# Shorter lags and another order of phases in the second attention's software pipeline

## The chip, the cores and the metric

The kernel runs on one core of one Trainium2 chip. The core has five engines with one instruction queue each: TensorE (PE in the profile; its weight loads are PEld), VectorE (DVE), ScalarE (ACT), GpSimd (POOL) and SyncE (SP, which here only issues DMAs). Each queue is worked off in its own order, and the queues wait for each other on semaphores. The metric is the device time of one launch in microseconds (us).

## The reference, cut to what matters

The program is one transformer chain on x of 32 sequences x 64 tokens x 256 features: a gated expert FFN, a hyperbolic attention, a typed expert FFN, a second attention with a router behind it, and a mixture-of-experts FFN. The change is in the second attention and its router:

```
x = x + _attn(x, ln1_w, ln1_b, conv_w, attn_w, proj_w, n_head)      # 16 heads of 16, RoPE, causal softmax
# inside _moe, what runs in the same stage of the kernel:
h = _layernorm(x, ln_w, ln_b)
logits = h @ router_w
expert_idx = jnp.argmax(logits, axis=-1)
```

## The kernel before, in words

`attention` is called twice, with the tag `hyp` (hyperbolic) and with the tag `rope` (the second attention; `hyper` is False). Its second half treats 16 blocks of 128 tokens (two sequences each) as items of a software pipeline. An item i goes through some 25 phases on five engines. The table `lag` says in which step of the pipeline: a phase of lag L treats item i in step i + L. The table `order` says in which order an engine issues its phases within a step. `run` issues steps 0 to `first` - 1 one by one, then a loop of two steps a turn up to step 15, then the remaining steps to 15 + the largest lag. With the largest lag 9 there are 25 steps, of which the loop holds 12 to 15. Most buffers are double, by the parity of the item.

The phases of the second attention, by engine, with the line that does the work:

- PE: `turn` (transposes of k, L1147, and q, L1153), `score` (q times k, L1169), `p_turn` (transposes of the probabilities, L1177), `mix` (probabilities times v, L1188), `y_turn` (L1200), `out` (output projection and residual, L1209 and L1211), `h_turn` (transposes of the normalised rows, L1227), `route` (router logits, L1239).
- ACT: copies out of PSUM, `q_blk` (L1251), `p_take` (L1284), `y_take` (L1289), `x2` (the sum x, L1295), `h_take` (L1309); `prob` (exponential, L1279); `rstd` (1/sqrt of the variance, two instructions, L1301 and L1303).
- DVE: `k_blk` (k spread into blocks by head, L1332), `clamp` (scale and causal mask, L1343), `top` (row maximum, L1354), `y` (division by the sum, L1360 and L1368), `stats` and `aggr` (mean and variance, L1380 and L1388), `keep` (logits to SBUF, L1393). Behind the last item `router.choose` (from L704 on) picks the experts.
- POOL: `shift` (minus the maximum, L1417), `total` (L1428), `norm` (L1432), `weigh` (L1438), `lift` (L1444). The last four make an item's rows for the expert stage.
- SP: loads `bring` (q and k, L1111), `fetch` (v, L1105), `bring_sum` (residual, L1116), `bring_x` (L1121) and `store` (rows to DRAM, L1127).

What the steps of the argument wait for: `h_turn(i)` waits for `lift(i)` and shares a PSUM bank with q's transposes; `total(i)` waits for `rstd(i)`, which waits for `aggr(i)`; `x2(i)` waits for `out(i)`; `q_blk(i)` waits for q's transposes of i; `score(i)` for `q_blk(i)`, `k_blk(i)` and `clamp(i-1)`; `out(i)` also for `bring_sum(i)`; `fetch(i)` for `mix(i-2)`, since it overwrites its buffer; and `p_turn(i)` for `prob(i)`. In the loop `score`'s waits stand on the last matmul of `route` (`score_ready`). The expert stage begins behind a barrier of all engines.

Of the kernel before, what the change touches and what calls it, by code (L numbers as in the profile page):

```python
# [17 lines left out]
KC = D // P  # L18
# [7 lines left out]
NP = N // P  # L26
# [687 lines left out]
def attention(nc, m, tag, hyper, srcT, resT, w, router=None, stored=None):  # L714
# [14 lines left out]
    with ExitStack() as s:  # L729
# [295 lines left out]
        if hyper:  # L1025
            lag = dict(turn=0, q_blk=0, k_blk=0, score=0, clamp=1, root_sq=1, root_ln=2, root=2, root_add=2, dist_ln=2,
                       dist=3, mask=3, top=3, shift=3, prob=4, p_turn=4, p_take=4, mix=5, y=5, y_turn=5, y_take=6,
                       out=6, add=6, stretch=0, fetch=3)
            order = dict(tensor="mix out turn p_turn y_turn score",
                         scalar="y_take dist root_ln prob root q_blk root_sq p_take dist_ln",  # L1030
                         vector="stretch clamp y add k_blk top", gpsimd="mask root_add shift", sync="fetch")
        else:
            lag = dict(bring=0, turn=1, q_blk=1, k_blk=1, score=1, clamp=2, top=2, shift=2, prob=2, p_turn=3, p_take=3,
                       mix=3, y=3, y_turn=4, y_take=4, out=4, fetch=2, bring_sum=3, bring_x=5, x2=4, stats=5, aggr=5, rstd=5,
                       total=5, norm=5, weigh=5, lift=5, h_turn=8, h_take=8, route=9, keep=9, store=7)
            order = dict(tensor="h_turn y_turn p_turn turn out mix route score",
                         scalar="y_take h_take p_take rstd q_blk x2 prob",
                         vector="stats clamp top aggr k_blk y keep", gpsimd="shift total norm weigh lift",
                         sync="bring fetch bring_sum bring_x store")
        last = max(lag.values())  # L1040
        sem = StageSemaphores(nc, tag)
# [14 lines left out]
        with ExitStack() as s2:  # L1056
# [42 lines left out]
            with nc.Block() as block:  # L1099
# [34 lines left out]
                def _(pe):  # L1134
                    def turn(i, q, nth):


                        if hyper:
                            pe.wait_ge(stretched, i + 1)
                        else:  # L1140
                            pe.wait_ge(brought[q], 16 * (nth + 1))
                        chunk = lambda n: x[:, q, n * P:(n + 1) * P]
                        wait(pe, k_blocked, i)
                        if not hyper:
                            wait(pe, kept, i + lag["turn"] - lag["route"])
                        for c in range(KC):
                            ins = pe.transpose(kT_ps[:, c * P:(c + 1) * P], chunk(KC + c), m.ident)  # L1147
                        ins.then_inc(k_turned, 1)
                        wait(pe, q_taken, i)
                        if not hyper:  # L1150
                            wait(pe, h_taken, i + lag["turn"] - lag["h_turn"] + 1)
                        for c in range(KC):
                            ins = pe.transpose(qT_ps[:, c * P:(c + 1) * P], chunk(c), m.ident)  # L1153
                        ins.then_inc(turned, 1)
# [26 lines left out]
                    def mix(i, q, nth):  # L1181

                        pe.wait_ge(p_taken, i + 1)
                        pe.wait_ge(v_fetched[q], 16 * (nth + 1))
                        wait(pe, y_scaled, i)
                        for hp in range(HP):
                            for j in range(2):
                                ins = pe.matmul(y_ps[j * T:(j + 1) * T, hp * 2 * VW:(hp + 1) * 2 * VW],  # L1188
                                                pT[:, q, hp, j * T:(j + 1) * T],
                                                v_now[:, q, j, hp].rearrange("p h v -> p (h v)"), start=True, stop=True)  # L1190
                        ins.then_inc(mixed, 1)
# [28 lines left out]
                    def h_turn(i, q, nth):  # L1220

                        pe.wait_ge(lifted, i + 1)
                        wait(pe, h_taken, i)
                        behind = i + lag["h_turn"] - lag["turn"]
                        wait(pe, q_taken, behind if not isinstance(i, int) else min(behind, NP))
                        for c in range(KC):
                            ins = pe.transpose(hT_ps[:, c * P:(c + 1) * P], router.rows[:, q, c * P:(c + 1) * P], m.ident)  # L1227
                        ins.then_inc(h_turned, 1)

                    def route(i, q, nth):  # L1230

                        pe.wait_ge(h_taken, i + 1)
                        wait(pe, kept, i)
                        behind = i + lag["route"] - lag["turn"] + 1
                        wait(pe, k_blocked, behind if not isinstance(i, int) else min(behind, NP))
                        for c in range(KC):
                            if not isinstance(i, int) and c == KC - 1:
                                score_ready(i + lag["route"] - lag["score"])
                            ins = pe.matmul(lg_ps, router.hT[:, q, c], router.wr[:, c], start=(c == 0), stop=(c == KC - 1))  # L1239
                        ins.then_inc(routed, 1)  # L1240

# [1200 lines left out]
```

## Time and profile before

| | us |
|---|---|
| median of 3 runs (2227.89 to 2228.91) | 2228.83 |
| the profiled execution's own time | 2227.89 |
| its span | 2226.1 |
| PE busy in the span | 2035.3 (91%) |
| DVE, ACT, POOL busy | 1106.0, 935.9, 720.6 |
| second attention's pipeline, first transposes to the last logits' copy | 1875.7 to 1987.4 |

The span is cut by stage: the pipeline of the second attention takes some 112 us of it, 5%. Busy shares of the whole program say little of it; its own stretch has to be read. Starts in the rows are us from the span's start.

### The profile page before, as it was taken

How to read it: one execution, taken by the hardware profiler on the slowest of the kernel's cores; microseconds unless marked ns; L12 is line 12 of the kernel's file. 1: busy time of each engine (PE TensorE's matmuls, PEld its weight loads, DVE VectorE, ACT ScalarE, POOL GpSimd, SP SyncE). 2: the span in 40 equal slices, each digit the busy share in tenths (PEclk: the TensorE clock that was granted, in tenths of full speed). 3: DMA queues.
4: the chain of work that ended last, by engine and by line, in shares of the span. 5: the costliest groups of instructions: out<-in, count | busy, mean ns of one | idle time of the engine just before them, and what ended most of it. 6: DMA issues, size and time to landing. Idle time of an engine off the chain costs nothing. (4 is left out here: it accounts for less than half of the span.)

```text
span 2226.1 us, 32462 instructions
## 1 busy us (share of the span) xinstructions
PE 2035.3 (91%) x11700; PEld 1717.9 (77%) x11700; DVE 1106.0 (50%) x1946; ACT 935.9 (42%) x1916; POOL 720.6 (32%) x777
## 2 busy tenths in 40 slices
PE   7999999999999999999998767799899765968998
PEld 6888888888888888888887545678699734858998
DVE  3334433443343344344344787333377574856775
ACT  4242323324233232323323599322255354645664
POOL 3030200203021020302200198202178314868884
PEclk9999999999999999999999798999999877978999
DMA  4010010101001010110000200320056303446661
GB/s 162 1 57 1 1 57 0 57 0 51 6 0 57 0 57 0 39 43 0 1 1 19 67 31 37 117 76 10 0 182 208 103 16 109 172 165 214 211 216 55
DMA packets 97922, 144.50 MB, mean 65 GB/s; under 512 B 15567, under 2 KB 72817, under 8 KB 97841
## 3 DMA queue, kind: packets, MB, share of 16 engines
q1 hardware_dynamic: 90784, 127.42, 17.7%
q0 software_dynamic: 4928, 12.86, 1.6%
q10 hardware_dynamic: 2128, 3.15, 0.4%
q8 instruction: 50, 0.82, 0.1%
q14 instruction: 32, 0.25, 0.0%
HBM read 109.32 MB, written 12.06 MB: 55 GB/s over the span
## 5 line engine op out<-in xcount | busy, mean ns | idle before, releaser
L584 DVE TENSOR_TENSOR cond_h<-cond_silu,ps 128x512 f32<-128x512 f32 x288 | 198.1, 688 | 696.5 <-ACT cond_silu L495 693.1
L495 ACT ACTIVATE cond_silu<-ps 128x512 f32<-128x512 f32 x288 | 172.3, 598 | 771.7 <-PE ps L414 771.7
L414 PE MATMUL ps<-a_x_hi,cond_w_hi 128*128 128x512 f32 x1152 | 449.3, 390 | 2.0 <-DVE a_x_lo L262 2.0
L414 PE MATMUL ps<-a_x_lo,cond_w_hi 128*128 128x512 f32 x1152 | 448.9, 390 | 0.0
L414 PE MATMUL ps<-a_x_hi,cond_w_lo 128*128 128x512 f32 x1152 | 448.7, 390 | 0.0
L383 POOL TENSOR_TENSOR cond_w_lo<-cond_stage_up,cond_w_hi 128x256 fp32r<-128x256 f32 x144 | 108.6, 772 | 832.3 <-ACT cond_w_hi L476 832.3
L414 PEld LDWEIGHTS ps<-a_x_hi,cond_w_hi 128*128 128x128 f32 x1152 | 216.7, 188 | 47.3 <-DVE a_x_lo L262 2.4
L414 PEld LDWEIGHTS ps<-a_x_hi,cond_w_lo 128*128 128x128 f32 x1152 | 216.6, 188 | 45.2
L414 PEld LDWEIGHTS ps<-a_x_lo,cond_w_hi 128*128 128x128 f32 x1152 | 216.7, 188 | 44.9
L430 PE MATMUL ps<-cond_h_hi,cond_d_hi 128*128 128x512 f32 x576 | 224.5, 390 | 3.4 <-DVE cond_h_lo L552 3.4
L430 PE MATMUL ps<-cond_h_hi,cond_d_lo 128*128 128x512 f32 x576 | 224.1, 389 | 0.0
L430 PE MATMUL ps<-cond_h_lo,cond_d_hi 128*128 128x512 f32 x576 | 224.1, 389 | 0.0
L552 DVE TENSOR_TENSOR cond_h_lo<-cond_h,cond_h_hi 128x512 fp32r<-128x512 f32 x288 | 199.7, 694 | 0.1
L489 ACT ACTIVATE cond_h_hi<-cond_h 128x512 fp32r<-128x512 f32 x288 | 179.6, 624 | 0.3 <-DVE cond_h L584 0.3
L430 PEld LDWEIGHTS ps<-cond_h_hi,cond_d_hi 128*128 128x128 f32 x576 | 108.1, 188 | 27.4 <-issue 2.4
L430 PEld LDWEIGHTS ps<-cond_h_hi,cond_d_lo 128*128 128x128 f32 x576 | 108.1, 188 | 22.6
L430 PEld LDWEIGHTS ps<-cond_h_lo,cond_d_hi 128*128 128x128 f32 x576 | 108.1, 188 | 22.3
L2024 POOL TENSOR_TENSOR moe_w_lo<-moe_stage_up,moe_w_hi 128x512 fp32r<-128x512 f32 x88 | 113.0, 1302 | 29.2 <-ACT moe_w_hi L2130 28.8
L555 DVE SCALAR_TENSOR_TENSOR dense_h_lo<-ps,dense_h_hi 128x512 fp32r<-128x512 f32 x64 | 44.2, 692 | 123.0 <-ACT dense_h_hi L501 123.0
L2077 PE MATMUL ps<-moe_x_hi,moe_w_hi 128*128 128x256 f32 x352 | 100.9, 287 | 1.4 <-DVE moe_x_lo L2185 1.4
L2077 PE MATMUL ps<-moe_x_lo,moe_w_hi 128*128 128x256 f32 x352 | 100.6, 286 | 0.0
L2077 PE MATMUL ps<-moe_x_hi,moe_w_lo 128*128 128x256 f32 x352 | 100.6, 286 | 0.0
(369 smaller groups left out, 4105.4 us busy)
## 6 DMA issues: line engine op xcount, KB each, us to landing
moe_stage_up<-in_L_ffn_expert_wv SPq DMA_DIRECT2D x22, 1024.0 KB, 8.2
typed_stage_up<-in_L_cond_wi SPq DMA_DIRECT2D x11, 1024.0 KB, 4.9
typed_stage_dn<-in_L_cond_wo SPq DMA_DIRECT2D x11, 1024.0 KB, 5.9
moe_stage_dn<-in_L_ffn_expert_proj SPq DMA_DIRECT2D x11, 1024.0 KB, 6.8
cond_stage_up<-in_L_cond_Wg SPq DMA_DIRECT2D x7, 1024.0 KB, 4.8
cond_stage_up<-in_L_cond_Wu SPq DMA_DIRECT2D x7, 1024.0 KB, 6.8
cond_stage_dn<-in_L_cond_Wd SPq DMA_DIRECT2D x7, 1024.0 KB, 5.4
hyp_v_now<-hyp_v_blk SPq DMA_DIRECT2D x16, 272.0 KB, 2.3
```

Of the source, the lines that this page charges most:

```text
L383: ins = pool.tensor_tensor(w_lo[:, j, :, c], stage_up[:, j, :, c], w_hi[:, j, :, c], ALU.subtract)
L414: ins = pe.matmul(up_ps[st % 2][j], w[:, j, k, fs], x[:, k, tok], start=(i == 0), stop=(i == 3 * KC - 1))
L430: ins = pe.matmul(y_ps[tt % 2][c], w[:, f, cs], x[:, st % HB], start=(f == 0 and i == 0), stop=(f == FC - 1 and i == 2))
L489: act.activation(h_hi[:, st % HB], h[:, st % 2], ACT.Copy).then_inc(h_rounded, 1)
L495: act.activation(silu[:, st % 2], up_ps[st % 2][0], ACT.Silu).then_inc(act_done, 1)
L552: dve.tensor_tensor(h_lo[:, st % HB], h[:, st % 2], h_hi[:, st % HB], ALU.subtract).then_inc(h_ready, 1)
L555: dve.scalar_tensor_tensor(h_lo[:, st % HB], up_ps[st % 2][0], 0.0, h_hi[:, st % HB], ALU.max, ALU.subtract).then_inc(h_ready, 1)
L584: dve.tensor_tensor(h[:, st % 2], silu[:, st % 2], up_ps[st % 2][1], ALU.mult).then_inc(up_free, 1)
L2024: pool.tensor_tensor(w_lo[:, :, :, fs(f)], stage_up[:, q, :, :, fs(f)], w_hi[:, :, :, fs(f)], ALU.subtract).then_inc(up_ready, 1)
L2077: ins = pe.matmul(up_ps[f % UB][j], w[:, j, k, fs(f)], x[:, q, k], start=(i == 0), stop=(i == 3 * KC - 1))
```

## The change

For the second attention alone, `lag` and `order` are other numbers and words. The lags of the router's phases fall (`h_turn` and `h_take` 8 to 6, `route` and `keep` 9 to 6, `store` 7 to 6), those of `fetch` 2 to 1 and `bring_x` 5 to 4. The largest lag is then 6: 22 steps, of which the loop holds 8 to 15. On PE `out` comes before `turn`, `h_turn` behind `p_turn`, `score` before `route`. On ACT `x2` and `q_blk` come before `rstd`. On DVE `clamp` comes before `stats`. In the loop `score`'s waits stand on the last matmul of `mix`. The waits that guard shared PSUM banks are written with the numbers that the new lags ask for.

```diff
-            lag = dict(bring=0, ..., fetch=2, bring_sum=3, bring_x=5, x2=4, stats=5, aggr=5, rstd=5,
-                       total=5, norm=5, weigh=5, lift=5, h_turn=8, h_take=8, route=9, keep=9, store=7)
-            order = dict(tensor="h_turn y_turn p_turn turn out mix route score",
-                         scalar="y_take h_take p_take rstd q_blk x2 prob",
-                         vector="stats clamp top aggr k_blk y keep", gpsimd="shift total norm weigh lift",
+            lag = dict(bring=0, ..., fetch=1, bring_sum=3, bring_x=4, x2=4, stats=5, aggr=5, rstd=5,
+                       total=5, norm=5, weigh=5, lift=5, h_turn=6, h_take=6, route=6, keep=6, store=6)
+            order = dict(tensor="y_turn p_turn h_turn out turn mix score route",
+                         scalar="y_take p_take h_take x2 q_blk rstd prob",
+                         vector="clamp stats top aggr k_blk y keep", gpsimd="shift total norm weigh lift",
...
-                            wait(pe, kept, i + lag["turn"] - lag["route"])
+                            wait(pe, kept, i - 5)
...
-                            wait(pe, h_taken, i + lag["turn"] - lag["h_turn"] + 1)
+                            wait(pe, h_taken, i - 4)
...
+                                if not hyper and not isinstance(i, int) and (hp, j) == (HP - 1, 1):
+                                    score_ready(i + lag["mix"] - lag["score"])
                                 ins = pe.matmul(y_ps[j * T:(j + 1) * T, hp * 2 * VW:(hp + 1) * 2 * VW],
...
-                        wait(pe, q_taken, behind if not isinstance(i, int) else min(behind, NP))
+                        wait(pe, q_taken, i + 5 if not isinstance(i, int) else min(i + 5, NP))
...
-                        wait(pe, k_blocked, behind if not isinstance(i, int) else min(behind, NP))
+                        wait(pe, k_blocked, i + 6 if not isinstance(i, int) else min(i + 6, NP))
                         for c in range(KC):
-                            if not isinstance(i, int) and c == KC - 1:
-                                score_ready(i + lag["route"] - lag["score"])
                             ins = pe.matmul(lg_ps, router.hT[:, q, c], router.wr[:, c], start=(c == 0), stop=(c == KC - 1))
```

ACT's queue in one full step, written out ahead of the loop. Before (`router_x2` is written by `x2`, `rope_qT` by `q_blk`, `router_rstd` by `rstd`):

```order
L1289 ACTIVATE rope_yT<-ps 128x256
L1309 ACTIVATE router_hT<-ps 128x256
L1284 ACTIVATE rope_pT<-ps 128x1024
L1301 ACTIVATE router_rstd<-router_mean,router_eps 128x1
L1303 ACTIVATE router_rstd<-router_rstd 128x1
L1251 ACTIVATE rope_qT<-ps 128x256
L1295 ACTIVATE router_x2<-ps 128x256
L1279 ACTIVATE rope_prob<-rope_u 128x1024
```

and now:

```order
L1287 ACTIVATE rope_yT<-ps 128x256
L1282 ACTIVATE rope_pT<-ps 128x1024
L1307 ACTIVATE router_hT<-ps 128x256
L1293 ACTIVATE router_x2<-ps 128x256
L1249 ACTIVATE rope_qT<-ps 128x256
L1299 ACTIVATE router_rstd<-router_mean,router_eps 128x1
L1301 ACTIVATE router_rstd<-router_rstd 128x1
L1277 ACTIVATE rope_prob<-rope_u 128x1024
```

The two instructions of `rstd` moved from ahead of `q_blk` and `x2` to behind both, and `router_hT` from ahead of `rope_pT` to behind it.

PE's queue in one full step. Before (`router_rows` is read by `h_turn`, `rope_x` by `turn`, `router_hT` by `route`):

```order
L1227 MATMUL ps<-const,router_rows 128x128 x2
L1200 MATMUL ps<-const,rope_y 128x128 x2
L1177 MATMUL ps<-const,rope_prob 128x128 x8
L1147 MATMUL ps<-const,rope_x 128x128 x2
L1153 MATMUL ps<-const,rope_x 128x128 x2
L1209 MATMUL ps<-rope_wo,rope_yT 128x256 x2
L1211 MATMUL ps<-const,router_res 128x128 x2
L1188 MATMUL ps<-rope_v_now,rope_pT 64x34 x16
L1239 MATMUL ps<-router_wr,router_hT 128x4 x2
L1169 MATMUL ps<-rope_k_blk,rope_qT 64x256 x8
```

and now:

```order
L1202 MATMUL ps<-const,rope_y 128x128 x2
L1177 MATMUL ps<-const,rope_prob 128x128 x8
L1228 MATMUL ps<-const,router_rows 128x128 x2
L1211 MATMUL ps<-rope_wo,rope_yT 128x256 x2
L1213 MATMUL ps<-const,router_res 128x128 x2
L1147 MATMUL ps<-const,rope_x 128x128 x2
L1153 MATMUL ps<-const,rope_x 128x128 x2
L1190 MATMUL ps<-rope_v_now,rope_pT 64x34 x16
L1169 MATMUL ps<-rope_k_blk,rope_qT 64x256 x8
L1237 MATMUL ps<-router_wr,router_hT 128x4 x2
```

`h_turn` moved from the front of the step to just ahead of `out`, and the item that it transposes is that of six steps ago, not of eight. `turn` stands behind `out`.

SP's queue at the pipeline's start, now:

```order
L1111 DMA rope_x<-rope_qk 128x512
L1105 DMA rope_v_now<-rope_v_blk 128x544
L1116 DMA router_res<-sum 128x2x128
L1111 DMA rope_x<-rope_qk 128x512
L1105 DMA rope_v_now<-rope_v_blk 128x544
L1116 DMA router_res<-sum 128x2x128
L1121 DMA router_x<-typed_table 128x256
```

The kinds of rows stand in the same order as before; what moved is the item of `rope_v_now` in a step (one later than before), and with it the `mix` that the row waits for, and all rows behind it.

## Rows read from the trace of the kernel before

**Rows 1.** Windows: steady part and drain; busy us (instructions), granted clock, DMA share.

```profile
core 0: us, PE busy (x) PEld busy (x) DVE busy (x) ACT busy (x) POOL busy (x), PEclk, DMA share, GB/s
1900.00:1965.40 65.40, 64.36 (x852) 54.14 (x848) 53.23 (x88) 42.25 (x88) 59.52 (x58) 1.00 0.49 171
1965.40:1987.40 22.00, 17.19 (x160) 14.87 (x156) 6.56 (x21) 9.12 (x24) 17.41 (x20) 0.86 0.34 116
```

**Rows 2.** Timeline, PE, one step in the loop: start, us, line, xcount, [idle before].

```profile
1941.95 0.44 PE L1227 MATMUL ps<-const,router_rows 128*128 128x128 f32 x2
1942.23 0.38 PE L1200 MATMUL ps<-const,rope_y 128*128 128x128 f32 x2
1942.44 1.04 PE L1177 MATMUL ps<-const,rope_prob 128*128 128x128 f32 x8
1943.32 0.38 PE L1147 MATMUL ps<-const,rope_x 128*128 128x128 f32 x2
...
1943.76 1.03 PE L1209 MATMUL ps<-rope_wo,rope_yT 128*128 128x256 f32 x4
...
1945.16 1.13 PE L1188 MATMUL ps<-rope_v_now,rope_pT 128*64 128x34 f32 x32
1946.21 0.61 PE L1239 MATMUL ps<-router_wr,router_hT 128*128 128x4 f32 x4
1946.75 1.09 PE L1169 MATMUL ps<-rope_k_blk,rope_qT 64*64 64x256 f32 x16
1947.78 0.44 PE L1227 MATMUL ps<-const,router_rows 128*128 128x128 f32 x2
```

**Rows 3.** Timeline, ACT, same step, one copy behind another.

```profile
1945.32 0.38 ACT L1251 ACTIVATE rope_qT<-ps 128x256 f32<-128x256 f32 x1
1945.60 0.38 ACT L1295 ACTIVATE router_x<-ps 128x256 f32<-128x256 f32 x1
```

**Rows 4.** Timeline, DVE and POOL, next step.

```profile
1948.00 1.23 DVE L1343 SCALAR_TENSOR_TENSOR rope_u<-ps,const 128x1024 f32<-128x1024 f32 x1 [0.17 <-PE ps L1169]
...
1949.42 1.22 DVE L1354 TENSOR_REDUCE rope_mx<-rope_u 128x16 f32<-128x1024 f32 x1 [0.19 <-DVE rope_u L1343]
...
1950.72 1.90 POOL L1417 TENSOR_TENSOR rope_u<-rope_u,rope_mx 128x1024 f32<-128x1024 f32 x1 [0.50 <-DVE rope_mx L1354]
...
1952.58 0.73 POOL L1428 TENSOR_TENSOR router_rows<-router_x 128x256 f32<-128x256 f32 x1
...
1955.40 0.73 POOL L1444 TENSOR_TENSOR router_rows<-router_xn,router_b 128x256 f32<-128x256 f32 x1
```

**Rows 5.** Timeline: hops from engine to engine, first in step 4, then in the drain.

```profile
1890.80 0.44 PE L1200 MATMUL ps<-const,rope_y 128*128 128x128 f32 x2
...
1891.27 0.38 ACT L1289 ACTIVATE rope_yT<-ps 128x256 f32<-128x256 f32 x1 [0.17 <-PE ps L1200]
...
1973.21 0.28 ACT L1301 ACTIVATE router_rstd<-router_mean,router_eps 128x1 f32<-128x1 f32 x1
...
1973.98 0.72 POOL L1428 TENSOR_TENSOR router_rows<-router_x 128x256 f32<-128x256 f32 x1 [0.46 <-ACT router_rstd L1303]
```

**Rows 6.** Timeline: k's blocks on DVE and the scores that wait for them.

```profile
1882.20 1.21 DVE L1332 TENSOR_TENSOR rope_k_blk<-ps,const 128x1024 f32<-128x1024 f32 x1
...
1883.51 1.98 PE L1169 MATMUL ps<-rope_k_blk,rope_qT 64*64 64x256 f32 x16 [2.73 <-DVE rope_k_blk L1332]
```

**Rows 7.** Timeline, SP's queue, a residual load; then the tile router_res: issue to landing.

```profile
1890.42 0.64 SPq L1116 DMA_DIRECT2D router_res<-sum  x1
...
DMA to landing us min/median/max: 2.2/2.3/3.9
```

**Rows 8.** Timeline: the last item's `lift`, its transposes, and the choice of experts.

```profile
1983.79 0.72 POOL L1444 TENSOR_TENSOR router_rows<-router_xn,router_b 128x256 f32<-128x256 f32 x1
1984.56 0.69 PE L1227 MATMUL ps<-const,router_rows 128*128 128x128 f32 x2 [2.16 <-POOL router_rows L1444]
...
1987.42 0.22 DVE L704 TENSOR_REDUCE router_best<-router_logits 128x16 f32<-128x64 f32 x1
```

**Rows 9.** Windows, a stretch of the first attention.

```profile
1328.00:1336.00 8.00, 5.45 (x71) 4.20 (x72) 7.10 (x9) 7.66 (x11) 7.39 (x4) 1.00 0.09 35
```

More of the change, by code:

```diff
@@ L1033, in attention @@
             lag = dict(bring=0, turn=1, q_blk=1, k_blk=1, score=1, clamp=2, top=2, shift=2, prob=2, p_turn=3, p_take=3,
-                       mix=3, y=3, y_turn=4, y_take=4, out=4, fetch=2, bring_sum=3, bring_x=5, x2=4, stats=5, aggr=5, rstd=5,
-                       total=5, norm=5, weigh=5, lift=5, h_turn=8, h_take=8, route=9, keep=9, store=7)
-            order = dict(tensor="h_turn y_turn p_turn turn out mix route score",
-                         scalar="y_take h_take p_take rstd q_blk x2 prob",
-                         vector="stats clamp top aggr k_blk y keep", gpsimd="shift total norm weigh lift",
+                       mix=3, y=3, y_turn=4, y_take=4, out=4, fetch=1, bring_sum=3, bring_x=4, x2=4, stats=5, aggr=5, rstd=5,
+                       total=5, norm=5, weigh=5, lift=5, h_turn=6, h_take=6, route=6, keep=6, store=6)
+            order = dict(tensor="y_turn p_turn h_turn out turn mix score route",
+                         scalar="y_take p_take h_take x2 q_blk rstd prob",
+                         vector="clamp stats top aggr k_blk y keep", gpsimd="shift total norm weigh lift",
                          sync="bring fetch bring_sum bring_x store")
@@ L1223, in h_turn @@
                         wait(pe, h_taken, i)
-                        behind = i + lag["h_turn"] - lag["turn"]
-                        wait(pe, q_taken, behind if not isinstance(i, int) else min(behind, NP))
+                        wait(pe, q_taken, i + 5 if not isinstance(i, int) else min(i + 5, NP))
                         for c in range(KC):
@@ L1233, in route @@
                         wait(pe, kept, i)
-                        behind = i + lag["route"] - lag["turn"] + 1
-                        wait(pe, k_blocked, behind if not isinstance(i, int) else min(behind, NP))
+                        wait(pe, k_blocked, i + 6 if not isinstance(i, int) else min(i + 6, NP))
                         for c in range(KC):
-                            if not isinstance(i, int) and c == KC - 1:
-                                score_ready(i + lag["route"] - lag["score"])
                             ins = pe.matmul(lg_ps, router.hT[:, q, c], router.wr[:, c], start=(c == 0), stop=(c == KC - 1))
```

## The prediction

> **What bounds the kernel now.** I read the windows of the second attention's pipeline first, since the change touches nothing else, then the timeline of all engines over one step, then the waits at its end. From 1900.0 to 1965.4 PE is busy 64.4 of 65.4 us at the full granted clock, POOL 59.5, DVE 53.2 [rows 1]: the steady part is bound by PE's own work. A step takes 5.83 us from one `h_turn` to the next, with row behind row: `h_turn` 0.28, `y_turn` 0.21, `p_turn` 0.88, `turn` 0.44, `out` 1.40, `mix` 1.05, `route` 0.54, `score` 1.03 [rows 2]. The drain behind the last scores, 22.0 us, is bound by something else: PE waits there for POOL's `lift` [rows 1, 8].
>
> POOL is late in a step. `shift` starts 2.9 us behind the end of the scores, and `total` to `lift` end at 1956.13 [rows 4], which is 2.4 us into PE's next step. Before, nobody minds: the item that POOL finishes there is transposed by `h_turn` three steps later.
>
> **The lag of `h_turn` is the first part.** It falls from 8 to 6, while `lift` stays at 5. So `h_turn` of step n+1 takes the item that POOL's queue finishes in its step n. It can start only behind `lift`, and `out`, `turn`, `mix` and `score` are queued behind it on PE.
>
> **The order on ACT is the second, and it closes a ring.** `rstd` stood ahead of `q_blk` and `x2`; now it stands behind them. ACT waits for `out` of the step (for `x2`) and for q's transposes (for `q_blk`) before it comes to `rstd`; POOL's `total` waits for `rstd`; `lift` comes three instructions later; and PE's next `h_turn`, ahead of the next `out`, waits for `lift`. Every step must thus go once around this ring, with start-to-start distances:
>
> - `h_turn` to `out`: 0.28, as `h_turn` took its place in the queue [rows 2].
> - `out` to the start of `q_blk`: out 1.40, k's transposes 0.22 (half of `turn`), q's transposes to ACT 0.47, the distance from `y_turn` to `y_take` of the same shape [rows 2, 5]. Sum 2.09. `x2` is done by then.
> - `q_blk` to `rstd`: 0.28, as from one such copy to the next [rows 3].
> - `rstd`'s first instruction to `total`: 0.77 [rows 5], the only place where POOL waits for it.
> - `total` to the end of `lift`: 3.55 (1952.58 to 1956.13) [rows 4].
> - end of `lift` to `h_turn`: 0.05 (1984.51 to 1984.56, where `h_turn` waited for it) [rows 8].
>
> Sum 7.02 us a step, against 5.83. Is there a later comer in it? `shift` must be done before `total`: scores end about 2.4 us ahead of the next `h_turn`, then 0.16, clamp 1.23, now `stats` 0.43, top 1.30 and shift 1.90 end 2.6 us behind `h_turn`, `total` starts 3.4 behind it: no. `k_blk` delays the scores: from k's transposes 0.47 + 1.21 + 0.10 [rows 5, 6] is 1.8 us, where PE with q's transposes and `mix` comes to the scores after 1.5. That is 0.3 us, but PE has 7.02 - 5.83 = 1.2 us of wait in each step in any case, so it is paid out of that. PE should wait about 0.8 us ahead of `h_turn` and 0.3 ahead of the scores.
>
> A rule on hops: the Trainium skill (Perfetto Trace Analysis, "Per-instruction lifecycle: what the profiler-reported window actually captures") says that the passing on of a semaphore lies outside the window that the profile reports. The rows agree: `rstd` is 0.28 and about 0.2 busy but `total` starts 0.77 behind its start. By busy times alone the ring would come to about 6.5 us and the sum below to some 8 us less; I go by starts.
>
> **SP's queue is the third.** `fetch` now stands for an item one later, so it waits for the `mix` of the same step, and `bring_sum` is queued behind it. In step 4 the residual load is issued at about 1890.4, behind `mix` of step 3, and lands 2.3 us later or a little more [rows 7], at 1892.9; PE wants it at 1892.1 (`y_turn` 1890.80, 0.36, `p_turn` 0.93). In step 5 the same costs again. Later the ring gives it time. Walked by the durations above: step 4 has `out` at 1892.9, k's blocks end 1.4 + 1.7 later, scores end at 1897.1. Step 5: `mix` ended 1895.8, residual issued 1896.4, lands 1898.7, `out` 1898.8; `shift` ends and `total` starts at 1902.1, `lift` ends 1905.65. The first `h_turn` thus is at 1905.7.
>
> **The sum.** From there ten rings to step 16 and one more to step 17: 11 x 7.02 = 77.2, at 1982.9. From step 17 no `turn` and no `q_blk` stand in the ring: `rstd` follows `x2` (1.51 behind the start of `out`: its 1.40 and a hop of some 0.1; then 0.28), so 0.28 + 1.51 + 0.28 + 0.77 + 3.55 + 0.05 = 6.44, three times: 2002.2. The last item has no `out` ahead of its `rstd`, but `h_take` of the item before stands there: 0.7 for `h_turn` at the lower clock [rows 8], then 0.3 + 0.77 + 3.55 + 0.05 = 5.4: 2007.6. From the last `h_turn` to the choice of experts took 2.86 [rows 8]; now `route` of the same item follows in the same step and does not wait for another item's, about 0.4 less: 2.45. The choice starts at 2010.0 instead of 1987.42: +22.6 us. What follows stands behind a barrier and shifts with it. The three steps fewer gain nothing, since the drain is a chain of POOL's work for the last items and not a count of steps. With the profiled execution's 2227.9 this gives 2250.5. The median of the three runs is 0.9 above that execution, so I keep 2250.5 within half a microsecond of either.
>
> **What I cost at nothing.** `clamp` ahead of `stats` moves the row maximum 0.25 us later in a queue (DVE) that has 12 of 65 us idle; hidden in the ring as shown. `bring_x` and `store` are issued one step earlier by number, but behind `fetch`; both have over 2 us until POOL wants them. The loop of eight steps in place of four: PE's step in the loop [rows 2] is as long as the sum of its rows, so no cost shows. The longer the ring, the more of this is covered. If ACT's or POOL's loop turns were not covered they would cost at most 0.3 us a step, +2.
>
> **Bounds.** The hop 0.77 is from one place; `q_blk` may start or hand over 0.1 earlier or later, `total` to `lift` 3.53 to 3.64. That makes 6.8 to 7.2 a step, -2.5 to +2.5 over the whole, and the tail +-1.5. The residual's delay is between 0 and 3 us (I take 1 in all).
>
> **Rivals.**
> - A: `rstd` is not late, so only `lift` to `h_turn` binds. Then two steps go from one scores' end by clamp, stats, top (3.1), shift to lift (5.4), `h_turn`, `out` (1.7), k's blocks (1.8) and scores (1.1), 13.1 in all, 6.55 a step. 11 x 0.47 less: 2245, with a tail 1.5 shorter 2244. For it speaks that `aggr` is early; against it that ACT works in order and `x2` must wait for `out`. 10%.
> - B, faster: the drain shrinks. The drain is 22.0 us [rows 1], of which four items' turns on POOL behind the last `shift` are 4 x 3.55 = 14.2. If the shorter lags let one of them be done earlier, 3.5 us are won, while 2 `h_turn` and 3 `route` (2.2 us) now come ahead of the last scores: 2226.6. This decides only if POOL never delays `h_turn`, that is if `lift` ends within 1.1 us of a step's start (`y_turn` and `p_turn`); it ends about 2.2 behind `y_turn`. 3%.
> - C, no change: PE stays the bound at 5.83 because the waits fit; 2228 +-4. It needs both of the above to be false. 2%.
> - D: the clock. PE gets gaps of about 1.2 in 7 us. In the first attention PE was busy 5.45 of 8 us and kept the full clock [rows 9], so I expect 1.0 in the steady part. If it fell to the lower level of 1.2 GHz, PE's 5.83 us would be about 11.7 a step and the end near 2290. In the drain (steps 19 to 21) it may fall, as before behind 1980; +1 to +2. 3% for the whole. The Trainium skill (TensorE: Matmul & The Clock Gate, "What's actually happening") says that the default state is the throttled one and that activity releases it; by that rule D would come if these gaps counted as idleness, and the row of the first attention speaks against it here.
>
> **How the numbers follow.** My forecast has 82%, A 10, B 3, C 2, D 3. Its own range is 2246 to 2255. The range 2243 to 2256 takes in A. A change is told from none at about 0.2%, 4.5 us: slower 0.95, the same 0.025, faster 0.025.
>
> **What would show it.** Pipeline step 7.0 us from one `h_turn` to the next, constant; POOL idle 0.8 us ahead of each `total`, put down to ACT `rstd`; PE idle ahead of `h_turn`, put down to POOL `lift`; ACT idle ahead of `x2`, put down to PE; granted clock 1.0 up to about 1990; the expert choice at 2010; everything before 1890 and all of the other stages unchanged in length. It would be wrong if `total` followed `shift` without a gap (A), or if PE's rows stood without a gap (C).

## The result, and the profile after

The changed kernel takes 2254.17 us (median of 4 runs, 2251.99 to 2255.2), the kernel before 2228.87 on the same chip (4 runs, 2227.89 to 2230.4): ratio 1.0112 (95%: 1.0098 to 1.0127). It is slower by 25.3 us. The forecast was 2250.5 with a range of 2243 to 2256.

The profiled execution took 2254.86 us, 27.0 more than that of before. Of this 2.1 us lie ahead of the second attention: its first transposes start at 1877.79 instead of 1875.69. No line that runs there was changed, and in other kernels below the same point falls between 1875 and 1881. So I compare the *pipeline*: from the first transposes to the choice of experts (L704) in the profiled execution. It grew from 111.73 to 136.70 us, by 25.0.

The first part of the profile of after has totals much as before, and tells little of where 25 us went:

```profile
PE 2045.2 (91%) x11700; PEld 1723.7 (77%) x11700; DVE 1107.6 (49%) x1946; ACT 940.5 (42%) x1916; POOL 721.1 (32%) x777
```

The windows of after over ten whole steps of the pipeline, and over its drain (columns as in [rows 1]):

```profile
1907.59:1979.63 72.04, 62.45 (x760) 50.70 (x760) 47.76 (x80) 39.30 (x80) 52.78 (x50) 1.00 0.41 142
1984.05:2014.49 30.44, 16.88 (x145) 14.03 (x144) 6.39 (x21) 8.92 (x23) 17.70 (x20) 0.76 0.27 92
```

PE was 64.36 of 65.40 us busy in the steady part [rows 1]; now no engine is near full. That is what a *ring* looks like: a closed chain of waits, from one step's work on an engine through the others and back to the same engine in a later step, so that all wait for each other in turn. The granted clock held 1.00 (the 2.4 GHz level) all the same and fell only in the drain. The waits view of after for the same ten steps (engine, line, waited for: us in total, times, longest) names both sides:

```profile
POOL rope_u L1415 <- DVE rope_mx L1352: 15.2, 10, 2.2
ACT router_x L1293 <- PE ps L1213: 10.1, 10, 1.7
DVE router_logits L1391 <- PE ps L1237: 9.6, 10, 1.0
PE ps L1228 <- POOL router_rows L1442: 8.4, 10, 1.2
```

The last line is the forecast gap ahead of `h_turn`: 0.84 us a step. The second, ACT's idle time ahead of `x2`, was forecast too. The first and third were not, and lead to what I missed. The timeline of after over two steps, only the rows of the two chains (start, us, engine, line, [idle before]):

```profile
1950.91 0.43 PE L1228 MATMUL ps<-const,router_rows 128*128 128x128 f32 x2 [0.89 <-POOL router_rows L1442]
...
1953.08 1.23 DVE L1330 TENSOR_TENSOR rope_k_blk<-ps,const 128x1024 f32<-128x1024 f32 x1 [0.30 <-PE ps L1147]
...
1954.61 1.09 PE L1169 MATMUL ps<-rope_k_blk,rope_qT 64*64 64x256 f32 x16
...
1955.63 0.61 PE L1237 MATMUL ps<-router_wr,router_hT 128*128 128x4 f32 x4
...
1956.38 0.16 DVE L1391 COPY router_logits<-ps 128x4 f32 x1 [0.95 <-PE ps L1237]
1956.49 1.23 DVE L1341 SCALAR_TENSOR_TENSOR rope_u<-ps,const 128x1024 f32<-128x1024 f32 x1
...
1958.23 0.44 PE L1228 MATMUL ps<-const,router_rows 128*128 128x128 f32 x2 [0.84 <-POOL router_rows L1442]
1958.23 1.22 DVE L1352 TENSOR_REDUCE rope_mx<-rope_u 128x16 f32<-128x1024 f32 x1 [0.19 <-issue]
1958.51 1.03 PE L1211 MATMUL ps<-rope_wo,rope_yT 128*128 128x256 f32 x4
...
1959.53 1.90 POOL L1415 TENSOR_TENSOR rope_u<-rope_u,rope_mx 128x1024 f32<-128x1024 f32 x1 [1.35 <-DVE rope_mx L1352]
...
1960.73 0.29 ACT L1299 ACTIVATE router_rstd<-router_mean,router_eps 128x1 f32<-128x1 f32 x1
...
1961.50 0.73 POOL L1426 TENSOR_TENSOR router_rows<-router_x 128x256 f32<-128x256 f32 x1
...
1964.33 0.72 POOL L1442 TENSOR_TENSOR router_rows<-router_xn,router_b 128x256 f32<-128x256 f32 x1
...
1965.27 0.43 PE L1228 MATMUL ps<-const,router_rows 128*128 128x128 f32 x2 [0.73 <-POOL router_rows L1442]
```

Two rings can be read off these rows.

*Ring 1*, the forecast one, closes in one step: `h_turn` 1958.23, `out` 0.28 later, `rstd` 2.22 later, `total` 0.77, end of `lift` (1965.05) 3.55, `h_turn` 0.22. Sum 7.04.

*Ring 2* closes in two steps. `keep` (the copy of the logits) is last in DVE's step. It waits for `route`, and `route` now stands behind `score` on PE. So the next `clamp`, whose scores ended at 1955.70, starts only behind `keep` at 1956.49, 0.8 later; before, 0.17 [rows 4]. From there `top` 1.74 later, `shift` 1.30, `total` 1.97, the end of `lift` 3.55, `h_turn` 0.22; and from the `h_turn` of 1950.91 to `route` 4.72 (through `out`, `turn`, `k_blk` at 1953.08 and the scores that wait for it), to `keep` 0.75, to `clamp` 0.11. Sum 14.36 for two steps, 7.18 for one. Both sums are by construction distances between two `h_turn`s; that each ring binds has to be shown by opening it, below.

At the `total` of 1961.50 both arrive together (`shift` ends 1961.43, `rstd` + 0.77 is 1961.50). In the step before `shift` was last: it ended at 1954.66, `total` is at 1954.62, and `rstd` had begun at 1953.48.

The mean of the eleven steps from 1907.59 to 1986.55 is 7.18, but they are not alike: 6.82, then 7.82, then seven of the loop with a mean of 7.22 (6.92 to 7.48), then 6.88 and 6.92 behind the loop. So ring 2 sets the step inside the loop only. There `top` starts 1.74 us behind `clamp` (1956.49 to 1958.23), behind the loop 1.47 (1978.32 to 1979.79), and in every second step `clamp` stands idle for 0.43 to 0.46 us behind `keep` with no releaser named:

```profile
1963.54 0.16 DVE L1391 COPY router_logits<-ps 128x4 f32 x1 [0.95 <-PE ps L1237]
...
1964.13 1.23 DVE L1341 SCALAR_TENSOR_TENSOR rope_u<-ps,const 128x1024 f32<-128x1024 f32 x1 [0.43 <-issue]
```

The drain of after, `h_turn`'s starts and what stood ahead of them, answering to [rows 8]:

```profile
1999.43 0.44 PE L1228 MATMUL ps<-const,router_rows 128*128 128x128 f32 x2 [2.37 <-POOL router_rows L1442]
1999.71 1.46 PE L1211 MATMUL ps<-rope_wo,rope_yT 128*128 128x256 f32 x4
...
2002.34 0.29 ACT L1299 ACTIVATE router_rstd<-router_mean,router_eps 128x1 f32<-128x1 f32 x1
...
2003.11 0.72 POOL L1426 TENSOR_TENSOR router_rows<-router_x 128x256 f32<-128x256 f32 x1 [3.74 <-ACT router_rstd L1301]
...
2006.70 0.69 PE L1228 MATMUL ps<-const,router_rows 128*128 128x128 f32 x2 [4.04 <-POOL router_rows L1442]
...
2012.08 0.69 PE L1228 MATMUL ps<-const,router_rows 128*128 128x128 f32 x2 [3.20 <-POOL router_rows L1442]
...
2014.49 0.22 DVE L704 TENSOR_REDUCE router_best<-router_logits 128x16 f32<-128x64 f32 x1
```

From `rstd` (2002.34) to `total` it is 0.77 again, as in [rows 5]. The granted clock was 1.00 up to 1998, 0.77 from 1998 to 2002 and 0.50 (the 1.2 GHz level) from 2002 on. The step that begins at 1999.43 is the first to feel it (`out` 1.46 instead of 1.03, the fall within it): it took 7.27 us where the two before took 6.44.

### The profile page after: what moved, and what is told of

The parts are those of the page before. It is cut to its first block and busy times, and to the rows that moved or that the text cites. A ratio compares the mean times of both kernels' runs of the same rounds, so it can differ in the third digit from the quotient of the medians.

```text
span 2253.1 us, 32560 instructions
## 1 busy us (share of the span) xinstructions
PE 2045.2 (91%) x11700; PEld 1723.7 (77%) x11700; DVE 1107.6 (49%) x1946; ACT 940.5 (42%) x1916; POOL 721.1 (32%) x777
## 5 line engine op out<-in xcount | busy, mean ns | idle before, releaser
L430 PEld LDWEIGHTS ps<-cond_h_hi,cond_d_hi 128*128 128x128 f32 x576 | 108.1, 188 | 27.4 <-issue 2.2
```

Of the source, the lines that this page charges most:

```text
L430: ins = pe.matmul(y_ps[tt % 2][c], w[:, f, cs], x[:, st % HB], start=(f == 0 and i == 0), stop=(f == FC - 1 and i == 2))
```

## The experiments

| kernel | pipeline, us | step, us | ratio (95%) |
|---|---|---|---|
| before | 111.73 | 5.83 | |
| after | 136.70 | 7.18 | 1.0112 (1.0098-1.0127) |
| lags alone | 139.12 | 7.16 (1929.07 to 1979.19; with the first three 7.30) | 1.0138 (1.0118-1.0158) |
| orders alone | 118.34 | 5.89 ahead of the loop, in it 6.5-6.9 | 1.0031 (1.0021-1.0041) |
| after, `rstd` early | 132.44 | 7.16 | 1.0110 (1.0093-1.0127) |
| after, `keep` moved | 135.92 | 7.02 | 1.0132 (1.0113-1.0151) |
| after, both | 128.64 | 6.74 | 1.0082 (1.0066-1.0099) |
| after, `fetch` lag 2 | 135.69 | 7.11 | a single run, 2252.34 us |
| after's orders, lags 8 | 147.03 | 7.1-7.6 and 10.2-11.3 in turn | 1.0164 (1.0147-1.0181) |
| the same, `store` 6 | 127.04 | 6.0-6.9 | 1.0065 (1.0049-1.0080) |
| before, ACT order of after | 125.34 | 7.28 | 1.0052 (1.0037-1.0067) |
| before, `rstd` late only | 113.33 | 5.83 | 1.0020 (1.0009-1.0031) |
| before, lags 7 and 8 | 111.24 | 5.83 | 0.9996 (0.9986-1.0005) |
| before, `norm` on DVE | 108.97 | 5.83 | 0.9992 (0.9983-1.0001) |

The ratios are against the kernel before on the same chip. The step of after and of the kernels made from it with lag 6 is the mean over the eleven steps from the first `h_turn`. The whole time scatters by some us with the stages ahead of the pipeline (15 runs of the kernel before on one chip took 2227.47 to 2233.3), so the step and the pipeline, each from one profiled execution, tell more than the ratio where it is a matter of 1 or 2 us.

**The two halves.** First, the kernel before with the lags of after and its own orders:

```diff
-  ... fetch=2, bring_sum=3, bring_x=5 ... h_turn=8, h_take=8, route=9, keep=9, store=7
+  ... fetch=1, bring_sum=3, bring_x=4 ... h_turn=6, h_take=6, route=6, keep=6, store=6
```

> The kernel before with all its orders, but the lags of the changed one. rstd is early, so there is no ring over ACT; h_turn stands first in the step and waits for the lift of the step before. Two-step ring: scores, clamp, top, shift to lift, h_turn, the whole step of 5.83, 14.2 us, 7.1 a step. In the drain rstd stands behind h_take: h_turn, h_take, rstd, total, lift, 5.2 us for each of the last four items instead of 3.55. Pipeline 111.7 + 14 + 6 = 131.5, 2248. If the lags alone cost little (only together with the late rstd): below 2238.

Measured: pipeline 139.12, +27.4; step 7.16 behind the first three. The step is as expected; the median, 2258.23 us, is 10 above the 2248 expected. The waits on PE from 1905 to 1970:

```profile
PE ps L1227 <- POOL router_rows L1444: 11.4, 8, 2.6
PE ps L1209 <- DMA router_res<-sum: 0.5, 1, 0.5
```

The pipeline is 7.6 us longer than expected. Some 1.6 of it is in the first two steps (7.48 and 8.32), most of the rest in the drain, whose first four steps took 8.07, 7.57, 8.14 and 5.89. The timeline, the rows of the first of them:

```profile
1979.19 0.61 PE L1227 MATMUL ps<-const,router_rows 128*128 128x128 f32 x2 [1.24 <-POOL router_rows L1444]
...
1981.97 1.03 ACT L1284 ACTIVATE rope_pT<-ps 128x1024 f32<-128x1024 f32 x1 [1.05 <-PE ps L1177]
1982.89 0.28 ACT L1301 ACTIVATE router_rstd<-router_mean,router_eps 128x1 f32<-128x1 f32 x1
...
1983.66 0.72 POOL L1428 TENSOR_TENSOR router_rows<-router_x 128x256 f32<-128x256 f32 x1 [1.19 <-ACT router_rstd L1303]
...
1986.48 0.72 POOL L1444 TENSOR_TENSOR router_rows<-router_xn,router_b 128x256 f32<-128x256 f32 x1
...
1987.26 0.44 PE L1227 MATMUL ps<-const,router_rows 128*128 128x128 f32 x2 [0.51 <-POOL router_rows L1444]
```

An early `rstd` still stands behind `p_take` on ACT, and `h_turn` ahead of `p_turn` on PE: 2.78 + 0.92 + 0.77 + 3.54 + 0.06 = 8.07 us. That is one more form of ring 1, here with a granted clock of 0.78 from 1980 to 2010. How much of it is the clock's wasn't separated. The `router_res` line above is one wait for the residual load.

Then the kernel before with the orders of after (and `score`'s waits on `mix`), its own lags:

```diff
-  tensor="h_turn y_turn p_turn turn out mix route score"
-  scalar="y_take h_take p_take rstd q_blk x2 prob"
-  vector="stats clamp top aggr k_blk y keep"
+  tensor="y_turn p_turn h_turn out turn mix score route"
+  scalar="y_take p_take h_take x2 q_blk rstd prob"
+  vector="clamp stats top aggr k_blk y keep"
```

> The kernel before with all its lags, but the orders of the changed one on PE, ACT and DVE, and score's waits on mix's last matmul. No ring through h_turn and no late residual load; q's transposes come behind out, so h_take is done when they want its bank. The step should be set by the two-step chain scores, route, keep, clamp, stats, top, shift, prob, p_turn, h_turn, out, turn, k_blk, scores, 12.6 us, 6.3 a step against 5.83: pipeline (first turn to choice) 111.7 + 11 x 0.47 = 117, 2234. If the orders were most of the change's cost: 2245 or more.

Measured: pipeline 118.34, +6.6, where 117 was expected. The size came out, but not as it was reasoned: no step has the 6.3 of the expectation. Ahead of the loop a step is 5.89; inside it 6.48 to 6.87, where the last matmul of `mix` takes `score`'s waits and stands behind `k_blk` (it names no releaser, but `k_blk` ends at 1947.32). From the timeline:

```profile
1946.13 1.19 DVE L1332 TENSOR_TENSOR rope_k_blk<-ps,const 128x1024 f32<-128x1024 f32 x1
...
1947.43 0.27 PE L1190 MATMUL ps<-rope_v_now,rope_pT 128*64 128x34 f32 x2 [0.48 <-issue]
```

Of the 6.6 us, 1.9 lie ahead of the first `h_turn`, 2.3 in the nine steps behind it and 2.4 in the rest.

The lags alone cost 27.4, the orders alone 6.6, both together 25.0. So the lags are the cause, taken as the set of seven that they are; that of `h_turn` was not shortened by itself. With the short lags the orders cost nothing more; the pipeline is 2.4 shorter. I read it so that ring-bound PE has idle time to pay for them; no run shows that by itself.

**The rings opened one by one.** After with `rstd` ahead of `x2` and `q_blk` (it stood behind `h_take`; the expectation puts it ahead of that too):

```diff
-  scalar="y_take p_take h_take x2 q_blk rstd prob"
+  scalar="y_take p_take h_take rstd x2 q_blk prob"
```

> The changed kernel, with rstd ahead of h_take and x2 in ACT's order again. Two theories. ONE RING: the step of 7.2 us is the ring h_turn, out, x2/q_blk, rstd, total, lift alone. Then the step falls to about 6.55 (lift behind shift behind the scores), and the drain, where rstd no longer waits for an out, by 9 us: 2254 - 7 - 9 = 2238. TWO RINGS: the trace of the changed kernel shows a second ring of nearly the same length over two steps: on DVE keep is the last phase of a step and waits for route, which now comes behind score, so the next clamp starts 0.8 us behind the scores instead of 0.16; clamp, stats, top, shift, total, lift, h_turn, out, turn, k_blk, score, route, keep is 14.2 us for two steps, 7.1. Then the step stays at 7.1 and only the drain is shorter by 9: 2244 to 2245.

Measured: step 7.16, as the theory of two rings says; if ring 1 alone had set the step, it would have fallen. The pipeline is 4.3 us shorter and not 9: the median is 2251.92 us, where 2244 to 2245 was expected. The drain gained less than expected: its steps became 6.21 and three of 5.12. They are again a ring over ACT: `h_turn` 0.47, `h_take` 0.30, `rstd` 0.77, `total` to `lift` 3.55, 0.05, sum 5.14. `rstd` had one more place to move, ahead of `h_take`.

After with `keep` one step later and behind `clamp`:

```diff
-  route=6, keep=6, store=6 ... vector="clamp stats top aggr k_blk y keep"
+  route=6, keep=7, store=6 ... vector="clamp keep stats top aggr k_blk y"
```

> The changed kernel, with keep one lag later (7) and right behind clamp in DVE's order, so that clamp no longer waits behind it for route. TWO RINGS: the second ring is opened, clamp starts 0.16 us behind the scores, the ring over ACT's rstd stays at 7.0: 0.15 us less in each of 11 steps, 2252 to 2253. ONE RING: nothing changes, 2254.

Measured: the step falls to 7.02. Behind 1925 the steps are 6.87 to 7.05; in after they are 6.88 to 7.48 there. The seven steps of the loop have a mean of 6.97, against 7.22, so `keep` cost 0.25 us a step in the loop, 1.8 in all, and nothing behind it. And now POOL waits for `rstd` in nearly every step, as the forecast had it (the waits view from 1925 to 1990, nine steps):

```profile
POOL router_rows L1426 <- ACT router_rstd L1301: 5.5, 9, 1.0
```

The pipeline is only 0.8 us shorter, since one of the last steps took 7.92, with a granted clock of 0.50 from 2001 to 2009. The median, 2258.22 us, is higher than after's and 5 above the 2252 to 2253 expected. In the profiled execution the pipeline began 3.5 us later than in after's (1881.3), so the ratio says nothing of this edit.

Both edits in one kernel:

> The changed kernel with both edits: rstd early on ACT and keep behind clamp on DVE. TWO RINGS: both are open; what is left is scores, clamp, keep, stats, top, shift, total, lift, h_turn, out, turn, k_blk, scores: 13.5 us over two steps, 6.75 a step, and the shorter drain: 2240 to 2241. ONE RING: the same as with rstd early alone (2238 if that is so).

Measured: step 6.74, as expected (6.75); pipeline 128.64. The median is 2246.63 us against 2240 to 2241 expected. The edits alone moved the step by 0.02 and 0.15; the two move it by 0.44. That is how two rings of nearly one length behave, and shows them both. In this kernel PE waits from 1910 to 1975 for the residual load too, the next limit:

```profile
PE ps L1211 <- DMA router_res<-sum: 2.1, 3, 1.1
PE ps L1228 <- POOL router_rows L1442: 1.6, 3, 0.6
```

**SP's queue.** After with `fetch` back at lag 2:

```diff
-  out=4, fetch=1, bring_sum=3
+  out=4, fetch=2, bring_sum=3
```

> The changed kernel with fetch at lag 2 again. The three waits of PE's out for the residual load (0.52, 0.57 and 0.52 us in steps 4, 5 and 7) go, the first h_turn comes about 1 us earlier from the first turn and the pipeline (first turn to choice of experts, 136.7 us) is 1.5 to 2 us shorter. The rings are untouched: 7.1 to 7.2 a step. If SP's order costs nothing, the pipeline stays at 136.7.

Measured: the first `h_turn` comes 28.9 us behind the first transposes instead of 29.8, and the second step takes 7.07 instead of 7.82: the third late load of after stood in it. That is 1.6 us, what PE waited for the load in after (1.6 us in three waits; here none). The pipeline is only 1.0 shorter, because one step of the drain took 7.93 at the lower clock (0.50 from 1996 on) instead of 7.27.

After's orders with lags of 8 and 7 for the router's phases:

```diff
-  h_turn=6, h_take=6, route=6, keep=6, store=6
+  h_turn=8, h_take=8, route=8, keep=8, store=7
```

> The changed kernel's orders on all engines, but h_turn, h_take, route, keep at lag 8 and store at 7, so h_turn takes an item whose lift ended two steps before. If the ring through h_turn is the cause, PE does not wait for lift any more: step 5.83 plus 0.3 for k_blk behind turn and the later clamp, 6.1 to 6.3, and a drain like before's: 2233 to 2237. If the orders alone were the cause (ACT's x2 and q_blk blocking rstd and prob), it stays near 2250.

Wrong by 27 us: 2264.1 us, slower than after, with steps of 7.1 to 7.6 and 10.2 to 11.3 in turn. The waits view of it from 1920 to 1990 has a line that after has not:

```profile
POOL router_rows L1426 <- DMA moe_table<-router_rows: 30.5, 7, 7.7
```

and the timeline shows SP's queue in front of it:

```profile
1933.92 1.13 PE L1190 MATMUL ps<-rope_v_now,rope_pT 128*64 128x34 f32 x32
1935.09 0.49 SPq L1105 DMA_DIRECT2D rope_v_now<-rope_v_blk  x1
1935.63 0.64 SPq L1116 DMA_DIRECT2D router_res<-sum  x1
...
1937.03 0.39 SPq L1127 DMA_DIRECT2D moe_table<-router_rows  x1
...
1940.72 0.72 POOL L1426 TENSOR_TENSOR router_rows<-router_x 128x256 f32<-128x256 f32 x1 [7.26 <-DMA moe_table<-router_rows]
```

With `fetch` at lag 1 SP stands behind `mix` of the step. The store is behind it in the queue, is issued at 1937.03, and `total` of the item after next, which overwrites the buffer, starts 3.7 us later. A third ring, over SP. The same kernel with `store` at lag 6:

```diff
-  keep=8, store=7
+  keep=8, store=6
```

> The run with the lags back at 8 had store at 7 too, and POOL's total waited there for the store's landing (30.5 us in all), because SP with fetch at lag 1 works a step later. Here h_turn, h_take, route and keep have lag 8, store stays at 6; all orders are the changed kernel's. RING: no wait for the store, none for lift; the step is set by scores, keep, clamp, stats, top, shift, prob, p_turn, out, turn, k_blk, scores, 12.6 us over two steps, 6.3, against 7.2 of the changed kernel and 5.83 of the one before; drain as before, 22 us: 2235 to 2239. If the lag of h_turn were not what matters, it would stay at 2250 or above.

Measured: the wait for the store is gone, pipeline 127.04, steps of 6.6 to 6.9 with two of 6.0 and 6.3, against an expected 6.3. The median is 2245.47 us, 6 above the 2235 to 2239 expected. The pipeline is 8.7 us longer than with the orders alone. Part of that is, from 1905 to 1975, the residual load behind `fetch`:

```profile
PE ps L1211 <- DMA router_res<-sum: 4.0, 6, 2.1
```

The rest wasn't separated; the loop holds six steps here and four there. So lags of 8 take 9.7 us off after's pipeline and leave 15.3 of the 25.0: with the ring through `h_turn` open, other limits come up, the late residual load and the orders (6.6) among them. The short lag of `h_turn` is not alone in what the change costs. And the change of `store` was not free to be left out: it belongs to that of `fetch`.

**ACT's order in the kernel before.** With the whole order of after:

```diff
-  scalar="y_take h_take p_take rstd q_blk x2 prob"
+  scalar="y_take p_take h_take x2 q_blk rstd prob"
```

> The kernel before, with nothing but the changed kernel's order on ACT (x2 and q_blk ahead of rstd, h_take behind p_take). If the order costs only because h_turn at lag 6 closes a ring through it, it costs nothing here but a later rstd in the drain: 0 to +1.5 us, 2228.5 to 2230. If a blocked ACT queue costs by itself (prob, and with it p_turn, behind x2 and rstd), every step gets longer by some 0.3 us: 2233 or more.

Wrong: 2241.99 us, pipeline +13.6, step 7.28. The waits from 1895 to 1965 name a neighbour that I had not thought of:

```profile
PE ps L1153 <- ACT router_hT L1309: 9.0, 7, 1.3
```

`h_turn` and q's transposes share a PSUM bank. `h_take` now stands behind `p_take` on ACT (1.0 us), and `turn` stands right behind `p_turn` on PE, so q's transposes wait for the bank. In after `out` stands between them and hides it. So this run did not test `rstd`. With `rstd` alone moved it does:

```diff
-  scalar="y_take h_take p_take rstd q_blk x2 prob"
+  scalar="y_take h_take p_take q_blk x2 rstd prob"
```

> The kernel before with rstd behind q_blk and x2 on ACT and nothing else; h_take stays ahead of p_take. The run with the whole ACT order cost 13.6 us because q's transposes wait for h_take (PE L1153 behind ACT L1309, 1.26 us in each step), h_take having moved behind p_take, not because of rstd. If so, this one costs nothing in the steps (rstd ends as shift does) and at most 0.7 us in the drain: 2228.5 to 2229.5, step 5.83. If a late rstd by itself holds up POOL and prob, the step is longer than 6.2 and it is 2233 or more.

Measured: the steps as before (5.82 to 6.00 from 1924 on), pipeline +1.6, all in the drain: there `rstd` stands behind the next item's `x2`, starts at 1978.00 instead of 1976.46 in before, and `total` at 1978.77 instead of 1977.48. A late `rstd` without a short lag of `h_turn` costs nothing in the steady part. That is read from one trace, of a run of 2229.36 us. The median of the eight runs is 2232.51, 3 us above the 2228.5 to 2229.5 expected; where the slower ones lose it no trace shows.

**How short may the lag be?** Before with `h_turn`, `h_take` 7 and `route`, `keep` 8:

```diff
-  h_turn=8, h_take=8, route=9, keep=9, store=7
+  h_turn=7, h_take=7, route=8, keep=8, store=7
```

> The kernel before with h_turn and h_take at lag 7 and route and keep at 8, nothing else: one step fewer, but still one step between lift (5) and h_turn. RING: lift ends 2.4 us into the step after its own and h_turn of lag 7 wants it a step later, so nothing waits; the step stays 5.83. One more h_turn and route (0.8 us) come ahead of the last scores, and the drain is POOL's four items as before: pipeline 112 to 113 us (111.7 before), 2228.5 to 2230. If shorter lags as such shorten the drain, a step's worth of some 3 us would be won: 2225. If lag 7 already closes a ring, the step is 6.2 or more and it is 2235 or more.

Measured: steps of 5.82 and 5.92 in turn, no wait of PE's matmuls for `lift` from 1905 to 1965, pipeline 111.24, ratio 0.9996 (0.9986 to 1.0005). In before's order the limit lies between these lags and the set with 6, and one step less in the table wins nothing that can be measured.

**A version for the drain.** Before, `norm` moved from POOL to the end of DVE's step (with it `total` no longer waits for `aggr` and `rstd`; those waits went over to `norm`):

```diff
-  vector="stats clamp top aggr k_blk y keep", gpsimd="shift total norm weigh lift"
+  vector="stats clamp top aggr k_blk y keep norm", gpsimd="shift total weigh lift"
```

> The kernel before, with norm moved from POOL to the end of DVE's step. In the drain POOL does four items of 3.5 us behind the last shift; without norm (1.22 on POOL) an item takes 2.3, until the last item's rstd (at 1979.6) sets the end: lift ends at about 1981.8 instead of 1984.5. DVE has 12 of 65 us idle in the steady part, and norm should take 0.3 to 0.5 of a step's 5.83. Expected 2 to 3 us faster, 2226. If DVE's longer queue delays clamp and with it p_turn, PE starts to wait in each step and it is 0 to 5 us slower.

Measured: pipeline 108.97, 2.8 us shorter; the step stays 5.83, and the last three `h_turn`s follow each other by 1.4 and 2.2 instead of 2.0 and 3.5. On DVE `norm` takes 0.41 us where POOL took 1.22 (1978.19 in before). How much of the gain comes from that and how much from the freed `total` wasn't separated:

```profile
1978.35 0.41 DVE L1396 TENSOR_SCALAR router_xn<-router_x,router_mean,router_rstd 128x256 f32<-128x256 f32 x1
```

The whole is 2226.82 us (11 runs) against 2228.4 (15), ratio 0.9992 (0.9983 to 1.0001). The lowest median of all, but its interval touches 1, so a gain is likely and not shown.

## Why the prediction was right in its mechanism, and what it missed

- **Sign and mechanism: right.** The lag of `h_turn` closes a ring through `lift`; PE waits 0.84 us ahead of each `h_turn` (0.8 forecast). With the lags alone it is there, with the orders alone it isn't. ACT's wait ahead of `x2` is there too (10.1 us in ten steps). The 0.3 us ahead of the scores are not: PE's only wait there is 0.7 us in four of ten steps.
- **The ring's length: 7.02 forecast, 7.18 measured**, over eleven steps 79.0 us against 77.2. Ring 1 by itself is right to 0.2: 6.82, 6.88 and 6.92 outside the loop, and 6.97 in it with ring 2 opened. The 1.7 us too much come from two places. The second step, 7.82, had a late residual load in it: the sentence "Later the ring gives it time" was wrong for one more step, and `fetch` put back takes 0.75 us off that step. And the seven steps of the loop have 7.22. There the sentence "Is there a later comer in it? ... no." failed. I took the scores' end and `clamp` 0.16 behind it, as before, and did not ask what else stood between them in DVE's queue. `keep` did, and it waits for a `route` that the change had moved behind `score`. "The loop of eight steps in place of four: ... no cost shows" failed with it: behind the loop the same order costs nothing, and I had read PE's rows for it and not DVE's.
- **Rival A was a real chain, priced too short.** Its 13.1 us for two steps are ring 2 without `route` and `keep`; with them and DVE's later `top` the trace has 14.36. I gave it 10% as if one ring had to be true and the other false; both were.
- **"POOL idle ahead of each `total`, put down to ACT `rstd`": true of some steps only.** The waits view has 2.3 us in three steps there (1907.59 to 1979.63); with `keep` moved it has 5.5 us in nine (1925 to 1990). In the others `shift` came last or with it.
- **"The order on ACT is the second, and it closes a ring": not needed for it.** The lags alone, with `rstd` early, reach the same 7.16. In the changed kernel either ring alone holds the step at 7.0 or above: 7.02 with ring 2 opened, 7.16 with ring 1 opened.
- **Start: right.** First `h_turn` 29.8 us behind the first transposes, 30.0 forecast; the residual load was late by 0.5 to 0.6 us in three steps, 1.6 in all, where the forecast had taken 1. With `fetch` put back, 0.9 us came back ahead of the first `h_turn` and 0.75 in the second step.
- **Drain: right but for the clock.** 6.44, 6.44, 7.27, 5.38 against 6.44 three times and 5.4; the last `h_turn` to the choice 2.41 against 2.45. I had named +1 to +2 us for a lower clock and left it out of the sum but for the last `h_turn`; it took 0.8.
- **"`bring_x` and `store` ... have over 2 us": true of this kernel**, because both lags fell with that of `fetch`. With the long lags of the router, `store` one step later costs 20.0 us (147.03 against 127.04). `bring_x` by itself wasn't tried.
- **Clock: right.** It stayed at 1.00 with PE busy 62.45 of 72.04 us. Rival D would have needed a fall here. Its price, twice 5.83 us, no row shows: at 0.50 `h_turn` took 0.69 us against 0.44 and `route` 1.01 against 0.61, less than twice as long.

Sum of the misses against the forecast of +22.6 for the pipeline: 1.7 in the eleven steps (0.8 in the second, 1.4 in the loop, -0.4 in the other three), 0.8 from the clock, -0.2 at the start, 25.0 measured (the rest is rounding). The remaining 2.1 us of the profiled execution arose ahead of the pipeline and isn't the change's. Whether it is of the placement of the code or of chance wasn't tried.

Left open: a kernel with the short lags, both rings open and the residual load early wasn't tried; the 6.74 us of the kernel with both edits are still 0.91 above PE's own step, so I expect nothing from it against before. Nor was a kernel tried in which `score`'s waits stand on `route`, or on no other matmul, with everything else of after.

## What to carry to other kernels

Before a lag in a software pipeline is shortened, ask when its producer ends and where its consumer stands in its queue. Here the lag of 7 left a whole step between them and won nothing that could be measured; the set with 6 made rings, and the step became the ring's length while no engine was full. Walk every ring, and put into it all that is queued ahead of a critical instruction, bookkeeping copies too, once for the straight steps and once for the loop. Of two rings of nearly one length, opening one gains next to nothing (0.02 and 0.15 us a step here, both together 0.44). Lags and orders that share a buffer or a PSUM bank belong together; taking some numbers back out of a consistent set can cost more than the whole set (35.3 us of pipeline against 25.0 here).

## What the runs showed of the hardware that I had not expected

- The clock: 1.00 over the 72 us of the ten steps, though PE stood idle ahead of each `h_turn`, 8.4 us in all. In the drain it was 1.00 from 1994 to 1998, with PE busy 2.78 of 4 us, 0.77 in the next 4 us (2.57 busy) and 0.50 from 2002 to 2006 (0.66 busy). The Trainium skill (TensorE: Matmul & The Clock Gate, "What's actually happening") says that activity releases the throttle; the rows agree in that the fall comes where PE begins to wait 2 to 4 us ahead of each `h_turn`.
- A stretch whose code is the same takes a few us more or less in another kernel: the pipeline's start lay at 1875.7 us in before, 1877.8 in after, 1881.3 with `keep` moved, and 1881.2 in before with lags 7 and 8. A difference of 2 us in the whole time of two such kernels is no evidence on the edit.
- In the loop the kernel with the orders alone takes 0.6 to 1.0 us a step more than ahead of it (6.48 to 6.87 against 5.89), with the same phases in the same order. Two things differ there: `score`'s waits stand on the last matmul of `mix`, and DVE is later, with `k_blk` 2.36 and 2.76 us behind `h_turn` (1946.13, 1953.01) instead of 1.95 (1927.39). What each costs wasn't separated.
